# Four edits to the prologue of an attention and mixture-of-experts kernel: an earlier turn of the first maxima, loads from another queue, a split table load, twenty unread products

## The chip, the cores and the metric

The kernel runs on one core of a Trainium2 chip. The metric is the device time of one execution in microseconds (us); lower is better. An execution is read through a hardware profile of the same program: what each engine did and when, what the DMA queues moved, and the clock that TensorE was granted.

## The reference

Two layers over x of shape (2, 1024, 128) in f32. Only the first is touched by the change: self-attention with 16 heads of 8 dimensions and a distance bias that falls with the head.

```python
qkv = x @ qkv_w.T + qkv_b                      # split per head into q, k, v of 8 columns
scores = einsum('bhid,bhjd->bhij', q, k) / sqrt(8) - |i - j| * 0.5**h
out = einsum('bhij,bhjd->bhid', softmax(scores), v) @ out_w.T + out_b
x = layernorm(x + out)
# second layer: layernorm, attention over pairs of tokens, top-2 of 8 experts
# with capacity 640 (gelu between two matmuls), weighted sum, residual, layernorm
```

## The kernel before

**Units.** The first attention is cut into 32 units (`UNITS`), each a few heads by some blocks of 128 queries; the first 24 have two heads. A unit's scores are computed twice. First come its eight "rows" (`max_half`): TensorE writes 128 queries by 1024 keys into a pair of PSUM banks (two pairs alternate), and VectorE reduces each pair to a row maximum (`reduce_row`). Then the scores are computed again, turned round, with the maxima subtracted inside the matmul (`exp_half`), ScalarE takes the exponent, and TensorE multiplies by the values (`values`). q and k are held as three bf16 parts, so that a product has 72 rows, to which rows for the distance and for the maxima are added. The diagonal block gets its distances from one more 128-column product with `slope_eye`.

**How maxima reach the second pass.** GpSimd splits a unit's eight maxima into three bf16 parts (`split_max`), VectorE turns the tile (`swap_max`), and SP's queue writes it to DRAM, waits until it has landed and loads it into rows of `q_stacks` (`load_max`). Unit 0 of the main loop starts when this is there, when unit 2's stacks are loaded, and when a pair of banks is free.

**The prologue.** TensorE turns the weights and x and makes eight projections (`project(y)`, 512 columns of f32). Pieces 0 to 2 go straight from SBUF into unit 0's stacks (`first_copies`, half of the copies from GpSimd's queue, half from SP's). Then TensorE waits, and runs the rows of units 0 and 1 (16 rows) with projections 4 to 7 and some weight transposes between them (`first_work`, after rows 3, 5, 7, 9 and 11). ScalarE evicts each projection in two operations (`project`, L1218 and L1224), and then copies the turned weights. VectorE's order is written out at the file's end: eight rows of unit m+2, with the turn of unit m+1's maxima after row index 2 of them. SP loads units 1 and 2 (`load_parts`, each two loads of q and two of k through DRAM) and then, in the loop, unit m+3 at unit m. GpSimd loads all slopes behind heads 0 to 3 in one transfer (L841) before it splits unit 0's maxima.

**The main loop.** For each of eight j, TensorE runs one row of unit m+2 and two halves of exponent input of unit m; after the second four it multiplies by the values. Waits are counted semaphores; every queue is in program order.

Of the kernel before, what the change touches and what calls it, by code (L numbers as in the profile page):

```python
# [12 lines left out]
P = 128  # L13
S = 2
N = 1024
D = 128
H = 16
DH = D // H
# [11 lines left out]
PARTS = 3  # L30
PRODUCTS = PARTS * PARTS * DH
# [4 lines left out]
SLOTS = 4  # L36
# [8 lines left out]
UNITS_C = H // 2  # L45
UNITS = NT // TC * UNITS_C
# [7 lines left out]
FOURS = 24  # L54
# [16 lines left out]
WEIGHT_DMAS = 4  # L71
FILLS = EXPERTS + TOP * NT // 8
SCATTERS = 2
LAST_GROUPS = ((0, 2), (2, 4), (4, 8), (8, 12), (12, 14), (14, 16))


# [100 lines left out]
def heads_in(m):  # L177

    return 4 if m >= FOURS else 2


def head_of(m, e):

    n = heads_in(m)
    u = m % (H // n)
    return 2 * n * (u // 2) + 2 * e + u % 2


def first_block(m):

    return NB // 2 + NB // 4 * ((m - FOURS) // SLOTS) if m >= FOURS else NB // 2 * (m // UNITS_C % 2)
# [17 lines left out]
def loads_by(m):  # L209

    return sum(loads_of(k) for k in range(m % SLOTS, m + 1, SLOTS))


def body(nc, t):

    with ExitStack() as ctx:
# [3 lines left out]
        def sem(name):  # L220
            return ctx.enter_context(nc.semaphore(name))
# [24 lines left out]
        k_late = sb("k_late", [P, H // 2, N], BF16)  # L246
# [66 lines left out]
        y_to = [sb(f"y_to{u}", [P, CT], U32) for u in range(2)]  # L313

        ld_w, ld_bias, ld_const, ld_slopes = sem("ld_w"), sem("ld_bias"), sem("ld_const"), sem("ld_slopes")
        ld_x = [sem(f"ld_x{g}") for g in range(NT // 4)]
        w_turned, w_kept = sem("w_turned"), sem("w_kept")
        x_turned, x_kept = sem("x_turned"), [sem(f"x_kept{g}") for g in range(NT // 4)]
# [74 lines left out]
        def queries(m, e):  # L393
            n = N // heads_in(m)
            return q_stacks[:, m % SLOTS, n * e:n * (e + 1)]

        def max_pair(k):

            first_bank = RING + 2 * (k % 2)
            return ps[:, first_bank:first_bank + 2, :]  # L400
# [15 lines left out]
        def first_copies(y, e):  # L416
# [3 lines left out]
            for i in range(PARTS):  # L420
# [4 lines left out]
                else:  # L425
                    yield k_stacks[to, 0, e, HALF * half:HALF * (half + 1)], parts[rows, y, :, :]

        def fetch_group(eng, g):

            lo, hi = LAST_GROUPS[g]  # L430
            eng.dma_start(got[:, lo:hi, :], yt.rearrange("(a p k) d -> p a (k d)", p=P, k=TOP)[:, lo:hi, :]
                          ).then_inc(fetched[g], 16)
# [17 lines left out]
        def _(sp):  # L450
# [15 lines left out]
                for out, src in first_copies(y, 1):  # L466
                    sp.dma_start(out, src).then_inc(loaded_direct, 16)

            def stack_of_four(m, rows):
                k = m % SLOTS  # L470
                if k < 2:
                    return k_late[rows, 4 * k:4 * (k + 1), :]
                return k_stacks[rows, 2 * (k - 2):2 * (k - 1), :, :].rearrange("r k e n -> r (k e) n")

            def load_tables(m):
                slot, n, h = m % SLOTS, heads_in(m), head_of(m, 0)
                if m < FOURS:
# [8 lines left out]
                if m >= FOURS or m % UNITS_C < SLOTS:  # L486
# [1 line left out]
                    sp.dma_start(q_stacks[ROW_ALIBI:ROW_MAX, slot, :].rearrange("r (e n) -> r e n", e=n),  # L488
                                 t["c_alibi_q"][:, first:first + N // n].unsqueeze(1).broadcast_to(
                                     [ROW_MAX - ROW_ALIBI, n, N // n])).then_inc(loaded[slot], 16)  # L490

            def load_parts(m):
                slot, s, n = m % SLOTS, m // (2 * UNITS_C), heads_in(m)
                first = P * first_block(m)
                for e in range(n):
                    sp.dma_start(queries(m, e)[0:PRODUCTS],
                                 q_dram[s, head_of(m, e), :, :, first:first + N // n].rearrange(
                                     "p d n -> (p d) n").unsqueeze(1).broadcast_to([PARTS * DH, PARTS, N // n])
                                 ).then_inc(loaded[slot], 16)
                    if n == 2:  # L500
                        sp.dma_start(k_stacks[0:PRODUCTS, slot, e, :],
                                     k_dram[s, head_of(m, e)].rearrange("d p n -> (d p) n").unsqueeze(0).broadcast_to(
                                         [PARTS, PARTS * DH, N])).then_inc(loaded[slot], 16)
                if FOURS <= m < FOURS + SLOTS:
                    h = head_of(m, 0)
                    for i in range(PARTS):
                        sp.dma_start(stack_of_four(m, slice(PARTS * DH * i, PARTS * DH * (i + 1))),
                                     k_dram[s, h:h + 7:2].rearrange("e d p n -> (d p) e n")).then_inc(loaded[slot], 16)

            def load_max(m):  # L510

# [31 lines left out]
                first_stack(y)  # L543
            for b in range(3):
                sp.wait_ge(parts_saved[b], SAVED[b])
            load_parts(1)
            load_parts(2)
            load_max(0)

            for m in range(UNITS):  # L550
                for c in range(LAST):
                    if m == first_unit(c + 1) + 1:
                        load_heads(c, 0, units_of(c) // 2)
                if m + 3 < UNITS:
                    if m > 0:
                        sp.wait_ge(ring_full, EXP_PLACE[m - 1, NB - 1, 1] + 1)
                    if m + 3 == UNITS_C:
                        sp.wait_ge(parts_saved[3], SAVED[3])
                    if m + 3 == 2 * UNITS_C:
                        sp.wait_ge(rest_saved, 16 * sum(1 if piece(y)[1] else PARTS for y in range(4, 8)))  # L560
                    load_tables(m + 3)
                    load_parts(m + 3)
                if m + 1 < UNITS:
                    load_max(m + 1)
                if m % 2 == 0 and m >= 2:
                    send_out(m // 2 - 1)
# [38 lines left out]
        def _(pool):  # L605
# [11 lines left out]
            for k in range(SLOTS):  # L617
                r = k % 2
# [46 lines left out]
            def split_max(m):  # L665
                b = m % 2
                src, rst, out = row_max[:, b, :], max_rest[:, b, :], max_parts[:, b, :]
                pool.wait_ge(mx_used, NB * m + NB)
                if m >= 2:
                    pool.wait_ge(max_swapped, m - 1)  # L670
                pool.tensor_tensor(out[:, 0:NB], src, no_bits[:], ALU.add).then_inc(split, 1)  # L671
                pool.wait_ge(split, 3 * m + 1)
                pool.tensor_tensor(rst, src, out[:, 0:NB], ALU.subtract).then_inc(split, 1)
                pool.wait_ge(split, 3 * m + 2)
                pool.tensor_tensor(out[:, NB:2 * NB], rst, no_bits[:], ALU.add).then_inc(split, 1)
                pool.wait_ge(split, 3 * m + 3)
                pool.tensor_tensor(out[:, 2 * NB:3 * NB], rst, out[:, NB:2 * NB], ALU.subtract).then_inc(max_split, 1)
# [160 lines left out]
            copy_v(1)  # L838
            copy_v(2)
            split_rest(3)  # L840
            pool.dma_start(slope_eye[:, 4:H, :], t["c_slope_eye"][4:H].rearrange("h p n -> p h n")).then_inc(ld_slopes, 16)  # L841
            split_max(0)
            split_rest(4)
            split_max(1)
            for m in range(UNITS):
# [30 lines left out]
        def _(pe):  # L876
# [219 lines left out]


            pe.wait_ge(ld_const, 16 * 3)
            pe.wait_ge(x_kept[3], 1)
            pe.wait_ge(first_loaded, 16 * 3 * PARTS)  # L1100
            pe.wait_ge(loaded[0], 16 * TABLES)
# [14 lines left out]
            pe.wait_ge(qf_ready, 8)  # L1116

            for m in range(UNITS):
                for group in range(2):
                    half = 2 * m + group  # L1120
                    for j in range(GROUP * group, GROUP * (group + 1)):
                        if j % 2 == 0:
                            for stage, c in hooks(half, (j % GROUP // 2,)):
                                late(stage, c)
                        if j == 0:
                            pe.wait_ge(max_loaded[m % SLOTS], 16 * turn_of(m))
                            if m + 2 < UNITS:
                                pe.wait_ge(loaded[(m + 2) % SLOTS], 16 * loads_by(m + 2))
                        if m + 2 < UNITS:
                            for h in range(2):  # L1130
                                max_half(m + 2, j, h)
                        for e in range(2):
                            exp_half(m, j, e)
                    for stage, c in hooks(half, (2,)):
                        late(stage, c)
                    if group == 1:
                        values(m, 0, half)
                    elif m > 0:
                        values(m - 1, 1, half)
# [65 lines left out]
        def _(act):  # L1205
# [50 lines left out]
            project(3)  # L1256
            act.wait_ge(loaded_direct, 16 * 3 * PARTS)
            act.wait_ge(first_loaded, 16 * 3 * PARTS)
            for y in range(4, 8):
                project(y)  # L1260
            act.wait_ge(late_turned, 1)
            act.copy(wo_t[:], ps[:, LATE_BANK, 0:P]).then_inc(late_kept, 1)
            act.copy(wq_t[:], ps[:, LATE_BANK, P:3 * P]).then_inc(late_kept, 1)
# [126 lines left out]
        def _(dve):  # L1390
# [277 lines left out]
            for m in range(-2, UNITS):  # L1668
                for i in range(NB):
                    if m + 2 < UNITS:  # L1670
                        reduce_row(m + 2, i)
                    if i == 2 and 0 <= m + 1 < UNITS:
                        swap_max(m + 1)
                    if i % GROUP == GROUP - 1 and m >= 0:
                        for stage, c in hooks(2 * m + i // GROUP):
                            late(stage, c)
# [147 lines left out]
```

## Time and profile before

| | us |
|---|---|
| median of 3 runs (606.59 to 613.73) | 608.09 |
| the profiled execution | 611.53 |
| its span, first to last instruction | 609.5 |
| TensorE busy | 525.3 (86% of the span) |
| VectorE busy | 404.4 (66%) |
| ScalarE busy | 340.3 (56%) |
| GpSimd busy | 216.9 (36%) |

Times in the profile run from the start of the span. PE is TensorE, DVE VectorE, ACT ScalarE, POOL GpSimd, SP the queue of SyncE; PEld is TensorE's weight load. A name with q behind it (SPq, ACTq) is an engine's DMA issue. In the chain of work that ended last, TensorE holds 71% of the span and VectorE 14%. TensorE's mean granted clock is 0.934 of full speed: 1.00 is 2.4 GHz and 0.50 is 1.2 GHz.

### The profile page before, as it was taken

To read this page: it belongs to the slowest core of one execution; us is meant where nothing else is said; L and a number is where in the kernel's file an instruction comes from. 1 tells how busy PE (TensorE), PEld (TensorE's weight loads), DVE (VectorE), ACT (ScalarE), POOL (GpSimd) and SP (SyncE) were. 2 spreads that over 40 slices of the span, in tenths; PEclk is the share of its full clock that TensorE was granted. 3 is DMA by queue.
4 is the path that set the end of the run, shared out by engine and by line. 5 is a ranking of instruction groups with operands and counts; after the bars stand their busy time and mean duration, and the time that the engine had idled before them with its cause. 6 is when DMAs were issued, how large, how long until landed. Compare 5 with 4: busy or idle time off the path is not lost.

```text
span 609.5 us, 11848 instructions
## 1 busy us (share of the span) xinstructions
PE 525.3 (86%) x4506; PEld 297.5 (49%) x4506; DVE 404.4 (66%) x688; ACT 340.3 (56%) x666; POOL 216.9 (36%) x404
## 2 busy tenths in 40 slices
PE   6579999999999999999999999999995219999910
PEld 4234444444444554544455455555663107888710
DVE  2697777787888667798865779987767612222217
ACT  4147676676767777756776676578691002332404
POOL 5735453111225215014701500470032740645540
PEclk9798999999999999999999999999997558999975
DMA  7622342322322323122222421111000121442124
GB/s 159 178 82 74 75 135 66 100 89 92 104 83 72 93 75 119 50 83 72 65 58 57 112 68 58 47 38 31 3 20 17 37 61 46 129 135 81 55 83 140
DMA packets 49191, 47.89 MB, mean 79 GB/s; under 512 B 13251, under 2 KB 38709, under 8 KB 49136
## 3 DMA queue, kind: packets, MB, share of 16 engines
q1 hardware_dynamic: 40800, 31.93, 19.0%
q0 software_dynamic: 5488, 12.73, 6.7%
q10 hardware_dynamic: 2848, 2.49, 1.3%
q8 instruction: 35, 0.57, 0.4%
q14 instruction: 20, 0.16, 0.1%
HBM read 31.67 MB, written 16.06 MB: 78 GB/s over the span
## 4 chain that ended last, share of the span: by engine, by line
PE 71%; DVE 14%; DMA 6%; POOL 3%; issue 3%; ACT 1%; another core or an unknown queue 1%; POOLq 0%; ACTq 0%; DVEq 0%; SPq 0%
PE ps L944 33%; PE ps L1004 17%; DVE row_max L1440 8%; PE ps L1160 6%; PE ps L1172 5%; PE ps L946 4%; POOL xd L831 2%; DMA max_dram<-max_turned 1%; DVE heads L1511 1%; PE ps L1044 1%; DVE x_tok L1730 1%; DMA k_stacks<-k_late 1%; PE ps L1149 1%; DMA q_stacks<-max_dram 1%
## 5 line engine op out<-in xcount | busy, mean ns | idle before, releaser
L1440 DVE TENSOR_REDUCE row_max<-ps 128x1 f32<-128x1024 f32 x256 | 297.3, 1213 | 89.7 <-PE ps L944 46.7
L1277 ACT ACTIVATE probs<-ps 128x512 f32<-128x512 f32 x512 | 268.3, 606 | 88.6 <-PE ps L946 47.1
L944 PE MATMUL ps<-k_stacks,q_stacks 96*128 96x512 bf16 x448 | 145.4, 389 | 12.8 <-DMA k_stacks<-k_late 5.9
L944 PE MATMUL ps<-q_stacks,k_stacks 99*128 99x512 bf16 (+1 forms) x512 | 142.4, 355 | 0.9 <-ACT probs L1277 0.5
L1004 PE MATMUL ps<-probs,v_unit 128*32 128x256 f32 x2048 | 123.8, 382 | 0.0
L946 PE MATMUL ps<-distance,slope_eye 128*128 128x128 bf16 x512 | 110.7, 222 | 0.0
L1004 PEld LDWEIGHTS ps<-probs,v_unit 128*32 128x32 f32 x2048 | 60.0, 109 | 51.5 <-issue 9.6
L944 PEld LDWEIGHTS ps<-k_stacks,q_stacks 96*128 96x128 bf16 x448 | 39.5, 99 | 82.0 <-DVE row_max L1440 28.3
L944 PEld LDWEIGHTS ps<-q_stacks,k_stacks 99*128 99x128 bf16 x512 | 48.7, 98 | 41.6 <-ACT probs L1277 12.1
L946 PEld LDWEIGHTS ps<-distance,slope_eye 128*128 128x128 bf16 x512 | 50.5, 99 | 25.8 <-issue 1.9
L1361 ACT ACTIVATE probs<-ps 128x640 f32<-128x640 f32 x32 | 22.5, 703 | 64.9 <-PE ps L1160 62.6
L867 POOL DMA_INDIRECT yt<-prod_mix,y_to x40 | 38.9, 972 | 52.9 <-DVE prod_mix L1699 41.9
L671 POOL TENSOR_TENSOR max_parts<-row_max,no_bits 128x8 bf16<-128x8 f32 x32 | 6.5, 202 | 130.7 <-DVE row_max L1440 128.7
L661 POOL COPY v_unit<-v_all 128x128 f32<-128x128 f32 (+1 forms) x28 | 8.5, 313 | 120.6 <-PE ps L1004 120.6
L1160 PE MATMUL ps<-probs,w 128*128 128x320 f32 x128 | 38.3, 455 | 1.2 <-DVE probs L1687 1.2
L831 POOL DMA_INDIRECT xd<-row_of,slot_u x32 | 31.8, 993 | 12.4 <-issue 11.0
L1172 PE MATMUL ps<-w,probs 128*128 128x128 f32 x280 | 32.4, 275 | 0.0
L1172 PEld LDWEIGHTS ps<-w,probs 128*128 128x128 f32 x280 | 31.8, 192 | 0.0
L1160 PEld LDWEIGHTS ps<-probs,w 128*128 128x128 f32 x128 | 24.1, 200 | 12.4 <-ACT probs L1361 3.3
L1686 DVE COPY columns<-probs 128x10 f32<-128x10 f32 x8 | 1.3, 164 | 37.5 <-PE ps L1149 30.8
L944 PE MATMUL ps<-q_stacks,k_late 99*128 99x256 bf16 x128 | 20.7, 272 | 0.0
L944 PE MATMUL ps<-k_late,q_stacks 96*128 96x512 bf16 x64 | 19.2, 381 | 1.2 <-DVE row_max L1440 1.2
(250 smaller groups left out, 444.4 us busy)
## 6 DMA issues: line engine op xcount, KB each, us to landing
k_stacks<-k_dram SPq DMA_DIRECT2D x46, 144.0 KB
q_stacks<-q_dram SPq DMA_DIRECT2D x46, 72.0 KB
w<-in_w SPq DMA_DIRECT2D x12, 256.0 KB
xd<-blank POOLq DMA_DIRECT2D x8, 325.0 KB, 2.8
probs<-xd SPq DMA_DIRECT2D x8, 325.0 KB
k_stacks<-in_c_alibi_k SPq DMA_DIRECT2D x24, 96.0 KB
out_dram<-out_t SPq DMA_DIRECT2D x16, 128.0 KB
yt<-zeros POOLq DMA_DIRECT2D x4, 512.0 KB, 3.0
```

The source lines that it names most:

```text
L661: pool.tensor_copy(v_unit[:, slot, :, 0:n, DH * r:DH * (r + 1)], v_all[:, first:first + 2 * n - 1:2, :, :].rearrange("p e j d -> p j e d") ...
L671: pool.tensor_tensor(out[:, 0:NB], src, no_bits[:], ALU.add).then_inc(split, 1)
L831: pool.indirect_dma_start(out=xd, out_offset=bass.IndirectOffsetOnAxis(ap=slot_u[c][:, k, j:j + 1], axis=0), in_=row_of[k][:, tiles(c)[j], ...
L867: pool.indirect_dma_start(out=yt, out_offset=bass.IndirectOffsetOnAxis(ap=y_to[u][:, a:a + 1], axis=0), in_=y_out[u][:, a, :], in_offset=N ...
L944: mm = pe.matmul(out, lhs, rhs, start=True, stop=at is None)
L946: mm = pe.matmul(out[:, at:at + P], slope_eye[:, head_of(m, e), :], distance[:], start=False, stop=True)
L1004: mm = pe.matmul(ps_o[32 * c:32 * c + 32, :], v_unit[:, m % SLOTS, j, c * heads_in(m) // 4, :], probs[:, (NB * m + j) % KEPT, QUARTER * c: ...
L1160: mm = pe.matmul(ps[:, 2 + 2 * (f % 2) + h, 0:CAP // 2], w1[u][:, f * P:(f + 1) * P], x_in_t[u][:, h * CAP // 2:(h + 1) * CAP // 2], start ...
L1172: mm = pe.matmul(ps[:, 6 + a // 4, (a % 4) * P:(a % 4 + 1) * P], act_t[u][:, f, a * P:(a + 1) * P], w2[u][:, f, :], start=(f == 0 and a % ...
L1277: act.activation(probs[:, k % KEPT, HALF * e:HALF * (e + 1)], ps[:, ring_of(n), :], ACT.Exp).then_inc(ring_read, 1)
L1361: act.activation(act_t[u][:, f, :].rearrange("p (h n) -> p h n", h=2), ps[:, 2 + 2 * (f % 2):4 + 2 * (f % 2), 0:CAP // 2], ACT.Gelu).then_ ...
L1440: dve.tensor_reduce(row_max[:, m % 2, i:i + 1], max_pair(k).rearrange("p a n -> p (a n)"), AX.X, ALU.max).then_inc(mx_used, 1)
```

## The change

Four edits, all ahead of the main loop or at its first passes.

1. `swap_max(0)` is called after the first row of unit 1 instead of the third.
2. `load_parts(2)` leaves SP's queue. ScalarE issues its four DMAs between `project(6)` and `project(7)`, behind a wait for unit 1's loads.
3. The slopes of heads 4 to 7 are loaded where heads 4 to 15 were; those of heads 8 to 15 after `split_max(0)`, and TensorE waits for them at unit 2 of the loop.
4. TensorE runs twenty 128x512 bf16 products into a PSUM bank that nothing reads, ahead of the waits for unit 0's stacks.

```diff
+IDLE_TURNS = 20
...
             for b in range(3):
                 sp.wait_ge(parts_saved[b], SAVED[b])
-            load_parts(1)
-            load_parts(2)
+            load_parts(sp, 1)
             load_max(0)
...
             split_rest(3)
-            pool.dma_start(slope_eye[:, 4:H, :], t["c_slope_eye"][4:H].rearrange("h p n -> p h n")).then_inc(ld_slopes, 16)
+            pool.dma_start(slope_eye[:, 4:8, :], t["c_slope_eye"][4:8].rearrange("h p n -> p h n")).then_inc(ld_slopes, 16)
             split_max(0)
+            pool.dma_start(slope_eye[:, 8:H, :], t["c_slope_eye"][8:H].rearrange("h p n -> p h n")).then_inc(ld_last_slopes, 16)
             split_rest(4)
...
             pe.wait_ge(ld_const, 16 * 3)
+            for _ in range(IDLE_TURNS):
+                pe.matmul(max_pair(0)[:, 0, :], distance[:], slope_eye[:, 0:4, :].rearrange("p h n -> p (h n)"),
+                          start=True, stop=True)
             pe.wait_ge(x_kept[3], 1)
...
             for m in range(UNITS):
+                if m == 2:
+                    pe.wait_ge(ld_last_slopes, 16)
...
-            for y in range(4, 8):
+            for y in range(4, 7):
                 project(y)
+            act.wait_ge(loaded[1], 16 * loads_by(1))
+            load_parts(act, 2)
+            project(7)
...
-                    if i == 2 and 0 <= m + 1 < UNITS:
+                    if i == (0 if m < 0 else 2) and 0 <= m + 1 < UNITS:
                         swap_max(m + 1)
```

`load_parts` and `stack_of_four` are moved out of SP's block unchanged, with the issuing engine as an argument.

## Rows read from the trace of the kernel before

**Rows 1.** Chain that ended last, 0 to 120 us: start us, length us, what.

```profile
24.64 0.59 PE ps L944
...
31.34 8.01 DVE row_max L1440 x7
39.50 1.97 DMA max_dram<-max_turned
41.48 2.58 DMA q_stacks<-max_dram
44.07 0.35 issue
```

**Rows 2.** Stretches: busy us (instructions) of PE, PEld, DVE, ACT, POOL; clock, DMA share, GB/s.

```profile
18.80:24.60 5.80, 0.00 (x0) 0.00 (x0) 1.17 (x6) 1.30 (x2) 5.36 (x10) 0.91 0.71 203
24.60:30.60 6.00, 5.60 (x14) 2.04 (x15) 4.70 (x4) 0.00 (x0) 2.08 (x3) 0.51 0.64 186
39.40:44.40 5.00, 2.67 (x13) 0.86 (x13) 5.00 (x6) 1.11 (x6) 2.30 (x4) 0.97 0.41 113
44.40:50.90 6.50, 6.48 (x23) 2.87 (x24) 4.43 (x5) 3.00 (x6) 5.04 (x13) 0.50 0.22 68
70.00:130.00 60.00, 59.01 (x536) 27.36 (x533) 45.50 (x45) 41.31 (x82) 20.24 (x43) 1.00 0.36 100
```

**Rows 3.** Timeline, VectorE: start us, length us, instruction [idle before, releaser].

```profile
25.79 4.82 DVE L1440 TENSOR_REDUCE row_max<-ps 128x1 f32<-128x1024 f32 x4 [5.82 <-PE ps L944]
...
39.39 5.71 DVE L1440 TENSOR_REDUCE row_max<-ps 128x1 f32<-128x1024 f32 x5
...
51.38 5.75 DVE L1440 TENSOR_REDUCE row_max<-ps 128x1 f32<-128x1024 f32 x5 [0.41 <-PE ps L944]
```

**Rows 4.** Timeline, TensorE: end of the x work, a projection at either clock.

```profile
16.70 2.02 PE L895 MATMUL ps<-w_t,qkv 128*128 128x128 f32 x16 [1.21 <-ACT qkv L1252]
...
29.14 1.67 PE L888 MATMUL ps<-qkv,w_t 128*128 128x512 f32 x2
...
31.64 1.02 PE L888 MATMUL ps<-qkv,w_t 128*128 128x512 f32 x2
```

**Rows 5.** Timeline, ScalarE and GpSimd: last evictions, copies, splits, DMA issues.

```profile
36.04 0.62 ACT L1224 CAST k_late<-heads 128x512 bf16<-128x512 f32 x1
37.58 0.69 ACT L1218 ACTIVATE heads<-ps,bias_q_scaled 128x512 f32<-128x512 f32 x1 [0.93 <-PE ps L888]
...
40.16 0.38 ACT L1268 COPY wv_t<-ps 128x64 f32<-128x64 f32 x2
...
25.62 1.06 POOL L841 DMA_DIRECT2D slope_eye<-in_c_slope_eye  x1
...
36.88 0.20 POOL L677 TENSOR_TENSOR max_parts<-max_rest,max_parts 128x8 bf16<-128x8 f32 x1
```

**Rows 6.** Timeline, SP's queue: issues of the units' loads.

```profile
24.11 0.79 SPq L496 DMA_DIRECT2D q_stacks<-q_dram  x1
...
29.68 0.71 SPq L501 DMA_DIRECT2D k_stacks<-k_dram  x1
...
42.28 0.51 SPq L478 DMA_DIRECT2D k_stacks<-in_c_alibi_k  x1
...
56.42 0.79 SPq L496 DMA_DIRECT2D q_stacks<-q_dram  x1
```

**Rows 7.** Short stretches: length, clock, DMA share, GB/s.

```profile
37.00:38.00 1.00, 1.00 0.09 33
38.00:39.00 1.00, 1.00 0.00 0
...
62.50:63.00 0.50, 1.00 0.20 74
...
64.00:64.50 0.50, 1.00 0.01 1
```

**Rows 8.** Chain, 78 to 96 us: the slowest trip of the maxima.

```profile
86.50 6.63 DMA max_dram<-max_turned
```

More of the change, by code:

```diff
@@ L315, in body @@
         ld_w, ld_bias, ld_const, ld_slopes = sem("ld_w"), sem("ld_bias"), sem("ld_const"), sem("ld_slopes")
+        ld_last_slopes = sem("ld_last_slopes")
         ld_x = [sem(f"ld_x{g}") for g in range(NT // 4)]
@@ L426, in first_copies, with stack_of_four, load_parts @@
                     yield k_stacks[to, 0, e, HALF * half:HALF * (half + 1)], parts[rows, y, :, :]
+        def stack_of_four(m, rows):
+            k = m % SLOTS
+            if k < 2:
+                return k_late[rows, 4 * k:4 * (k + 1), :]
+            return k_stacks[rows, 2 * (k - 2):2 * (k - 1), :, :].rearrange("r k e n -> r (k e) n")
+        def load_parts(eng, m):
+            slot, s, n = m % SLOTS, m // (2 * UNITS_C), heads_in(m)
+            first = P * first_block(m)
+            for e in range(n):
+                eng.dma_start(queries(m, e)[0:PRODUCTS],
+                             q_dram[s, head_of(m, e), :, :, first:first + N // n].rearrange(
+                                 "p d n -> (p d) n").unsqueeze(1).broadcast_to([PARTS * DH, PARTS, N // n])
+                             ).then_inc(loaded[slot], 16)
+                if n == 2:
+                    eng.dma_start(k_stacks[0:PRODUCTS, slot, e, :],
+                                 k_dram[s, head_of(m, e)].rearrange("d p n -> (d p) n").unsqueeze(0).broadcast_to(
+                                     [PARTS, PARTS * DH, N])).then_inc(loaded[slot], 16)
+            if FOURS <= m < FOURS + SLOTS:
+                h = head_of(m, 0)
+                for i in range(PARTS):
+                    eng.dma_start(stack_of_four(m, slice(PARTS * DH * i, PARTS * DH * (i + 1))),
+                                 k_dram[s, h:h + 7:2].rearrange("e d p n -> (d p) e n")).then_inc(loaded[slot], 16)
         def fetch_group(eng, g):
@@ L467, in first_stack @@
                     sp.dma_start(out, src).then_inc(loaded_direct, 16)
[L469 to L473, printed above, removed]
             def load_tables(m):
@@ L490, in load_tables @@
                                      [ROW_MAX - ROW_ALIBI, n, N // n])).then_inc(loaded[slot], 16)
[L492 to L508, printed above, removed]
             def load_max(m):
@@ L561, in _ @@
                     load_tables(m + 3)
-                    load_parts(m + 3)
+                    load_parts(sp, m + 3)
                 if m + 1 < UNITS:
```

## The prediction
> **What bounds the kernel now.** I read the page first: TensorE is busy for 86% of the span and holds 71% of the chain, so the middle is TensorE's. The windows by stretch say the same: 59.0 of 60 us busy from 70 to 130 us, at full clock [rows 2]. A loop so full starts later or sooner as a block, so what the prologue gives up passes on to the end nearly whole. Next I read the chain through the prologue. It enters the rows of unit 0 at 24.6 us, goes through the rows of units 0 and 1 at VectorE's pace, and then through the trip of unit 0's maxima: save 1.97 us, load 2.58, 0.35 of issue, so that TensorE enters the main loop at 44.07 + 0.35 = 44.42 us [rows 1]. Last I read the clock. It is 0.91 on average in the 5.8 us in which TensorE does nothing and 0.51 from 24.6 to 30.6. It falls again to 0.50 from 44.4 to 50.9 us, after five microseconds in which TensorE was busy for 2.67 of 5.00 [rows 2]. The reader is to see two prices: a late entry into the loop, and a slow first half unit behind it.
>
> **The unread products.** The last work on x ends at 16.70 + 2.02 = 18.72 us [rows 4], the first row starts at 24.64 [rows 1]. A product streams 512 columns: 0.213 us at 2.4 GHz, 0.427 at 1.2 GHz (columns over clock). Twenty take 4.3 us, to 23.0, and hide in the wait; wholly at the low clock they take 8.5, to 27.3, and cost 2.6. A mean clock of 0.91 over 5.8 us is a full one until about 23.6 although TensorE had stopped at 18.7 [rows 2], so I take 4.3 and cost them at nothing.
>
> What they buy: a row streams 512 + 128 + 512 columns, 0.96 us at the low clock and 0.48 at the full one. The first reduction started 25.79 - 24.64 = 1.15 us after the row [rows 1, 3]; at full clock 0.67, so 25.3. Reductions then follow at 8.01 / 7 = 1.144 us [rows 1]. The fifth would start at 25.3 + 4 x 1.144 = 29.9 us, against 31.34. It is fed in time: row 3 may start when row 1 is reduced, at 27.6; 0.48 for it, 1.02 for the projection behind it [rows 4], 0.67 for the next gives 29.8. **Gain 1.45 us.** If the clock is low again by then, the same sum is 27.6 + 0.96 + 1.67 + 1.15 = 31.4, gain nothing. TensorE works 3 rows x 0.48 in the first 2.5 us after 24.6, a poor load like the one before 44.4. I keep 0 and 1.45 as bounds and take 1.0 for the mean of executions; the sum below goes by 1.45, and says what the lower value does.
>
> **The turn two rows sooner.** Before, the eighth row is reduced at about 31.34 + 4 x 1.144 = 35.9, GpSimd's split starts right behind it and ends at 36.88 + 0.20 = 37.08 [rows 5], and the turn comes only at 39.3, just ahead of the reductions of 39.39 [rows 3]. After, it waits for the split alone: all 1.45 sooner, split done 35.65, ninth reduction done 35.7, turn done 35.9. VectorE stalls some 0.1 us, since the ninth reduction just covers the split. The save starts at 35.95 instead of 39.50, lands at 37.9, and the load at 40.5; with 0.35 of issue TensorE could start at 40.9. So this edge stops being the last. The next one late is the bank pair: unit 2's first row needs the reduction of the row two before, the fifteenth. Before, the sixteenth ended at 39.39 + 5.71 = 45.10, the fifteenth at 43.95; less 1.45 and plus the stall gives **42.6**, a gain of 1.8 if nothing else is later.
>
> **Unit 2's loads.** Here something is later. ScalarE ends `project(6)` at 36.04 + 0.62 = 36.66, now 35.2 [rows 5]. Four issues at SP's 0.79 [rows 6] take it to 38.3. `project(7)` and the weight copies follow; before they took from 37.58 to 40.16 + 0.38 = 40.54, 2.96 us [rows 5], so 41.3 us now, 1.3 under the 42.6 at which TensorE needs them. Hidden. But the loads themselves: unit 4's, alone, were issued from 56.42 and its traffic ended just before 64.0 [rows 6, 7], 7.4 us. From 35.2 that is **42.6 at the soonest**. Before, the same loads were issued by 29.68 + 0.71 and gone by 37.4 [rows 6, 7], 7 us ahead of their use; that slack is spent. And they aren't alone. GpSimd's second slopes load and its save of piece 4 fall into the stretch, and, since SP's `load_max(0)` is done 3.5 us sooner, SP goes on to unit 3's tables and loads at 39 instead of 42.28 [rows 6]. Units 1 and 2 together took 24.1 to 37.4, 13.3 us for two, so overlapping units delay each other: an extra of 0 to, at the extreme, 13.3 - 7.4 = 5.9 us. Unit 3's own large loads come only in the last two microseconds, so I take 1.0, near the lower end: landed 43.6, and with 0.35 of issue TensorE enters the loop at **43.95 instead of 44.42**. If the clock spoiled the first stretch, everything is 0.4 later and the entry is where it was.
>
> A transfer tail of this kind shows a DMA share of 0.20 at 74 GB/s [rows 7], that is about 3 of 16 engines: a k load runs on few engines, and adding another queue doesn't widen it. The Trainium skill, page "DMA: Bandwidth & Descriptors", section "Why a DMA increments its semaphore by 16 and not by 1", says that a copy is spread over the largest count up to 16 that divides its slowest dimension, the lowest-numbered engines first; k's is 3. The trace agrees with three.
>
> **The rest.** The second slopes issue costs GpSimd under the 1.06 us of the whole one [rows 5]; behind it stand `split_rest(4)` and then `split_max(1)`, which can't start before the sixteenth reduction. From 39.40 to 44.40 GpSimd was busy for 2.30 of 5.00 us [rows 2], so 2.7 us of idle time cover it. Hidden; without that cover unit 1's maxima would come 1.06 later, and they are wanted a whole unit after unit 0's. TensorE's wait for the last slopes is at loop unit 2, near 70 us, 30 us after the issue. Nothing.
>
> **Sum.** Entry 44.42 to 43.95: -0.5. Slow half unit behind it: unchanged. Span 609.5 to 609.0, the profiled execution 611.53 to 611.0. The median shown is 608.09, 3.4 below the profiled execution, so the same difference gives **607.6 us**.
>
> **Rivals.** (a) *The second slow stretch goes.* In the loop's first steps TensorE streams four products of 512 columns and three of 128, 2.03 us at 1.2 GHz and 1.01 at 2.4; at the low clock it sets the pace, at the full one VectorE does. The reduction of the loop's fourth row started at 51.38; at 1.144 us a row it would start at 45.1 + 3 x 1.144 = 48.5 [rows 3]. So 2.85 us hang on the clock. If the load lands at 42.6 the entry is 43.0, 1.4 sooner, and TensorE's lean stretch is shorter: -1.4 - 2.85 = -4.2, **603.9**. For it: the mean of 0.97 over the lean stretch [rows 2] says that the clock held for nearly all of it, and the cure comes with a small shift. Against: by my entry the lean stretch grows, from 5 us to nearly 6, since it now begins 1.45 sooner and ends only 0.5 sooner. Chance 0.25. A mild form, start sooner and clock kept in one execution of two, is about 605.5 and lies between.
>
> (b) *The loads make the entry later: slower.* Place: engines that carry unit 2's k, unit 3's first loads and the small load of the maxima at once. The slowest save of the maxima took 6.63 us instead of 1.97, with unit loads and weights in flight [rows 8]. Price: the entry is at load + 0.35, so it turns into a loss when unit 2's traffic needs more than 44.07 - 35.2 = 8.9 us, or when save and load together need more than 44.07 - 35.95 = 8.1 against 4.55 before. With 6.63 + 2.58 the entry is at 45.5, +1.1; with the load 3 us delayed, 46.0, +1.5: **609.4**. Chance 0.2. The same page of the Trainium skill, section "Queues, rings and completion order", says that an engine takes turns between its queues by whole packets of descriptors; were that so here, the many short pieces of the maxima would stand behind pieces of unit 2's k, and this rival is what it would give. No row of before has the two on different queues.
>
> (c) *The products are in the way.* If the clock is already low at 18.7, they end near 27.3 and the first row is 2.6 late: **610.5** after the 0.1 to 0.2 that comes back. Chance 0.05.
>
> (d) *Nothing passes on*, since the load alone sets the entry and takes all: 608.1. Chance 0.05.
>
> **Numbers.** My forecast, entry within about 1 us of before, has 0.45: its own range is 606.6 to 608.6. The range holds (a)'s nearer part and (b): 603.7 to 610.3, with (c) and the far side of (a) outside. A change of 2% is 12 us, about what a measurement of this kernel can tell from none; no case above comes near it, so faster 0.02, same 0.96, slower 0.02.
>
> **What would show it.** In the profile after: twenty products from 18.7 to 23.0 and a clock of 1.00 at 24.6 (else the first step is wrong); the fifth reduction at 29.9; the save of the maxima at 36.0; ScalarE's four issues from 35.2; and, as the release of the first row of the loop, a DMA of unit 2's stacks and not of the maxima, at 43.6. If the release is a reduction at 42.6, the loads were quick, and I was too dark; if the clock then holds at 1.00 from 44 to 51 us, (a) holds and the gain is about 4 us.

## The result: slower by 0.4%, and the profile after

The changed kernel takes 611.49 us at the median against 608.64 us, and the ratio is 1.0041 with an interval of 1.0023 to 1.0058, some 2.5 us. The forecast was 607.6 us, a gain of 0.5 us on the median known then. The profiled execution took 611.57 us, its span is 609.6 us, so the two profiled executions end alike: that of before was 2.9 us slower than its median, that of after was at its median. The two traces differ where the change is, and the difference can be followed from there to the end of the loop. The first view is the chain that ended last, cut to the prologue (start us, length us, what).

```profile
19.63 4.32 PE ps L1102 x20
23.94 0.67 issue
...
28.70 1.71 PE ps L890 x2
...
36.10 0.62 ACT k_late L1231
36.72 0.75 ACTq L440
...
39.11 8.91 DMA k_stacks<-k_dram
48.02 0.24 issue
48.26 0.58 PE ps L946
```

The twenty products take 4.3 us and end before the first row, as worked out. TensorE enters the loop at 48.26 us instead of 44.42 [rows 1], and what releases it is neither the trip of the maxima nor a reduction but unit 2's second k load, issued by ScalarE at 39.11 and landed 8.91 us later. From the first of the four issues to the landing it is 48.02 - 36.10 = 11.9 us; the same loads alone took 7.4 [rows 6, 7]. The queues' timeline shows who else was there, first ScalarE's queue and then SP's.

```profile
36.10 1.36 ACTq L440 DMA_DIRECT2D q_stacks<-q_dram  x1
...
39.11 0.73 ACTq L445 DMA_DIRECT2D k_stacks<-k_dram  x1
39.89 0.69 ACT L1225 ACTIVATE heads<-ps,bias_q_scaled 128x512 f32<-128x512 f32 x1 [3.17 <-issue]
```

```profile
37.42 0.37 SPq L516 DMA_DIRECT2D max_dram<-max_turned  x1
38.98 0.76 SPq L518 DMA_DIRECT2D q_stacks<-max_dram  x1
39.78 0.48 SPq L498 DMA_DIRECT2D k_stacks<-in_c_alibi_k  x1
...
42.06 0.71 SPq L445 DMA_DIRECT2D k_stacks<-k_dram  x1
...
43.63 0.71 SPq L445 DMA_DIRECT2D k_stacks<-k_dram  x1
```

Since the maxima turn sooner, SP is through with them at 39.7 us and goes on at once to unit 3: its two k loads are issued at 42.06 and 43.63, while both of unit 2's are on their way. Unit 3 is not wanted for another unit. The short stretches (length, clock, DMA share, GB/s) show what they share.

```profile
43.00:44.00 1.00, 1.00 0.85 275
44.00:45.00 1.00, 0.99 0.62 183
45.00:46.00 1.00, 0.50 0.25 94
46.00:47.00 1.00, 0.50 0.21 80
47.00:48.00 1.00, 0.50 0.19 74
```

A lone unit's load ends in a tail at a share of 0.20 and 74 GB/s [rows 7]. Here two units from two queues are in flight, and the tail is the same 0.20: the second queue adds no rate. From 46 to 48 us the traffic by queue (packets, MB, share of 16 engines; q1 is SP's, q0 GpSimd's, q10 ScalarE's) is:

```profile
q1 hardware_dynamic: 52, 0.08, 10.6%
q0 software_dynamic: 19, 0.05, 6.2%
q10 hardware_dynamic: 15, 0.02, 3.2%
```

The three together make up the 20%: SP's unit 3 and transfers of GpSimd take most of it, and the load that TensorE waits for gets the least. Unit 3's tail goes on alone to 50.9 us.

The timeline of VectorE (start, length, instruction, what ended the idle time) has the rest.

```profile
25.30 4.66 DVE L1450 TENSOR_REDUCE row_max<-ps 128x1 f32<-128x1024 f32 x4 [4.44 <-PE ps L946]
31.40 5.75 DVE L1450 TENSOR_REDUCE row_max<-ps 128x1 f32<-128x1024 f32 x5 [1.44 <-PE ps L946]
37.19 0.21 DVE L1458 STREAM_TRANSPOSE max_turned<-max_parts 128x32 bf16<-128x32 bf16 x1
...
49.42 1.23 DVE L1450 TENSOR_REDUCE row_max<-ps 128x1 f32<-128x1024 f32 x1 [4.13 <-PE ps L946]
...
54.01 5.71 DVE L1450 TENSOR_REDUCE row_max<-ps 128x1 f32<-128x1024 f32 x5
```

VectorE waits 4.13 us for the loop. The first row starts at a slightly different time in each execution, so I compare kernels by the time from the first reduction of all to the fourth reduction of the loop. Before it is 51.38 - 25.79 = 25.6 us [rows 3], after 54.01 - 25.30 = 28.7: **3.1 us lost in the prologue**. That is carried through: the last save of the maxima is issued at 442.74 us, 388.7 us after the fourth reduction, and before at 440.14, 388.8 after it. Between the loop and the end the profiled execution won back 2.5 us in work that no edit touches; the median did not.

The stretches of before, asked of after (busy us and instructions of PE, PEld, DVE, ACT, POOL; clock, DMA share, GB/s):

```profile
24.60:30.60 6.00, 4.69 (x15) 1.87 (x16) 4.66 (x4) 0.07 (x1) 3.79 (x6) 0.78 0.43 120
39.40:44.40 5.00, 2.95 (x16) 0.99 (x14) 5.00 (x6) 2.31 (x8) 3.21 (x5) 1.00 0.61 179
44.40:50.90 6.50, 2.64 (x10) 1.27 (x11) 2.11 (x2) 0.95 (x2) 4.86 (x13) 0.54 0.24 83
70.00:130.00 60.00, 58.97 (x554) 27.55 (x552) 44.73 (x44) 40.33 (x80) 22.63 (x47) 1.00 0.36 98
```

Against [rows 2], the first stretch has a clock of 0.78 instead of 0.51, the third has TensorE busy for 2.64 of 6.50 us instead of 6.48, and the loop is what it was.

### The profile page after: what moved, and what is told of

The parts are those of the page before. It is cut to its first block, busy times and chain, and to the rows that moved or that the text cites. A ratio compares the mean times of both kernels' runs of the same rounds, so it can differ in the third digit from the quotient of the medians.

```text
span 609.6 us, 11889 instructions
## 1 busy us (share of the span) xinstructions
PE 526.7 (86%) x4526; PEld 298.3 (49%) x4526; DVE 403.9 (66%) x688; ACT 340.2 (56%) x666; POOL 218.7 (36%) x405
## 4 chain that ended last, share of the span: by engine, by line
PE 70%; DVE 14%; DMA 6%; issue 3%; POOL 3%; ACT 2%; ACTq 0%; POOLq 0%; DVEq 0%; SPq 0%
PE ps L946 32%; PE ps L1006 16%; DVE row_max L1450 8%; PE ps L1167 6%; PE ps L1179 5%; PE ps L948 4%; POOL xd L832 2%; DMA k_stacks<-k_dram 1%; DVE heads L1521 1%; PE ps L1046 1%; DMA max_dram<-max_turned 1%; DVE x_tok L1740 1%; DMA w_nat<-in_qkv_w 1%; PE ps L1156 1%; PE ps L890 1%
## 5 line engine op out<-in xcount | busy, mean ns | idle before, releaser
L946 PE MATMUL ps<-k_stacks,q_stacks 96*128 96x512 bf16 x448 | 143.7, 386 | 12.3 <-DVE row_max L1450 5.5
L869 POOL DMA_INDIRECT yt<-prod_mix,y_to x40 | 38.9, 973 | 49.9 <-DVE prod_mix L1709 36.1
```

Source lines behind the costliest of these rows:

```text
L869: pool.indirect_dma_start(out=yt, out_offset=bass.IndirectOffsetOnAxis(ap=y_to[u][:, a:a + 1], axis=0), in_=y_out[u][:, a, :], in_offset=N ...
L946: mm = pe.matmul(out, lhs, rhs, start=True, stop=at is None)
```

## The experiments

Theory one: the loss is unit 2's loads alone. Their last issue is at 39.1 us instead of 29.7, and they share a few DMA engines with unit 3's loads, which the earlier turn of the maxima pulls forward. Theory two: the turn, the slopes, the products or ScalarE's queue as such cost the time. All ratios are to the kernel before on the same chip.

**Unit 2's loads back on SP's queue**, the other three edits kept.

```diff
             load_parts(sp, 1)
+            load_parts(sp, 2)
...
-            for y in range(4, 7):
-                project(y)
-            act.wait_ge(loaded[1], 16 * loads_by(1))
-            load_parts(act, 2)
-            project(7)
+            for y in range(4, 8):
+                project(y)
```

> The changed kernel with unit 2's loads back on SP's queue; the other three edits stay. Theory one (the late, shared loads of unit 2 are the whole loss): the first row of the loop is released by the reduction of the fifteenth row at about 42.6 to 43.5 us instead of by a DMA at 48.0, and the time falls 4 to 5 us below the changed kernel's, to a ratio of 0.992 to 0.998 of the kernel before. Theory two (the loss comes from the earlier turn, the split slopes or the products): the entry stays later than 44.4 us and the ratio at 1.002 or above.

Measured: 0.9984 (0.9966 to 1.0003), 5.7 thousandths below the changed kernel. The loss is gone; theory one holds for its place. The gain of 0.2% to 0.8% that I expected did not come whole. TensorE enters the loop at 42.59 us, where I expected it, but the first reduction was early too, at 23.99: between the two are 18.6 us, as in the kernel before. The timelines of VectorE and, last line, TensorE say why.

```profile
23.99 9.14 DVE L1448 TENSOR_REDUCE row_max<-ps 128x1 f32<-128x1024 f32 x8 [3.86 <-PE ps L947]
34.35 1.23 DVE L1448 TENSOR_REDUCE row_max<-ps 128x1 f32<-128x1024 f32 x1 [1.22 <-PE ps L947]
...
49.12 5.75 DVE L1448 TENSOR_REDUCE row_max<-ps 128x1 f32<-128x1024 f32 x5
```

```profile
33.64 0.39 PE L947 MATMUL ps<-k_stacks,q_stacks 96*128 96x512 bf16 x1 [1.19 <-DMA k_stacks<-k_dram]
```

Eight reductions now run without a gap, 9.14 us for eight; the products do keep the clock here. But the ninth row waits 1.2 us for unit 1's load: the rows have caught up with it. SP's save of the maxima, issued at 35.72, is followed by the load only at 38.92, 3.2 us for the save, with unit 2's loads ahead of it; it did not set the entry, since TensorE was still at the sixteenth row until 42.5 us. From the first reduction to the loop's fourth it is 25.1 us.

**Only ScalarE's issue of unit 2's loads**, on the kernel before.

```diff
+            act.wait_ge(loaded[1], 16 * loads_by(1))
+            load_parts(act, 2)
```

> The kernel before with one edit only: ScalarE's queue issues unit 2's loads between projections 6 and 7. Theory one: issue from 36.7 us, unit 3's loads follow 3 us later than in the changed kernel, so the overlap is smaller; landed at 44.5 to 47, entry at 45 to 47.5 and a ratio of 1.001 to 1.005. Theory two (this edit alone is harmless, since 7.4 us from 36.7 is 44.1, under the 44.07 of before or nearly): entry within 0.3 us of 44.42, ratio 1.000 +- 0.001.

Measured: 1.0066 (1.0047 to 1.0085), more than the whole change and more than either theory gave it. One edit makes the loss, and the other three win some of it back. The chain of this kernel:

```profile
40.10 3.45 DMA max_dram<-max_turned
43.57 2.81 DMA q_stacks<-max_dram
```

Here it was not the load of unit 2 that came last but the trip of the maxima: 6.3 us instead of 4.6 [rows 1], although nothing else was in SP's queue. The entry is at 46.76 us. So the late loads hurt in a second way: the small transfers of the maxima get slower beside them. That they share DMA engines with them is the likely reason; the trace doesn't name the engines of a single transfer. The trace gives 28.3 us to the loop's fourth reduction, 2.7 more than before; the ratio says 4 us, and that difference I can't place.

**Unit 3's loads held back** until unit 2's have landed, in the changed kernel.

```diff
+                    if m == 0:
+                        sp.wait_ge(loaded[2], 16 * loads_by(2))
                     load_tables(m + 3)
```

> The changed kernel with one wait more: SP holds unit 3's tables and loads back until unit 2's have landed. Theory one in its form that the two units' k loads share the same few DMA engines: unit 2's last load lands 7.4 to 8.8 us after the first issue, at 43.5 to 45, instead of 11.9 us after; entry at 44 to 45.3, 3 to 4 us sooner than in the changed kernel. Theory two (ScalarE's queue is slow by itself, or the slopes and the save of piece 4 are what it shares with): landing stays at 46 or later, entry 46.5 to 48.

Measured: 1.0029 (1.0014 to 1.0043). The queues and TensorE:

```profile
35.82 0.37 SPq L516 DMA_DIRECT2D max_dram<-max_turned  x1
40.13 0.76 SPq L518 DMA_DIRECT2D q_stacks<-max_dram  x1
42.49 0.32 SPq L498 DMA_DIRECT2D k_stacks<-in_c_alibi_k  x1
```

```profile
44.31 0.58 PE L948 MATMUL ps<-k_stacks,q_stacks 96*128 96x512 bf16 x1 [2.17 <-DMA q_stacks<-max_dram]
```

ScalarE's first issue was at 33.72, and at 42.49 unit 2 had landed: 8.8 us at most instead of 11.9. So unit 3's loads were 3 us of the delay, as theory one has it. Then the second way shows alone: the save takes 4.3 us and the load 3.8, and they set the entry at 44.31. GpSimd's new slopes load is issued 1.4 us ahead of this save and is a rival for its slowness. Two things speak against it: the run before this one has no such load and its save takes 3.45 us, and in five of the runs below, with cut k loads, the slopes load stands 0.3 us ahead of the save, which takes 1.4 to 2.0 us. Without unit 3 in the way the change is still no gain.

**Each k load cut into three transfers of 24 rows**, on all two-head units of the changed kernel (counts of awaited loads raised to match). A k load writes 72 rows from a source repeated three times, an outer size of 3.

```diff
-                    eng.dma_start(k_stacks[0:PRODUCTS, slot, e, :],
-                                 k_dram[...].unsqueeze(0).broadcast_to([PARTS, PARTS * DH, N]))
+                    for i in range(PARTS):
+                        eng.dma_start(k_stacks[PARTS * DH * i:PARTS * DH * (i + 1), slot, e, :],
+                                     k_dram[s, head_of(m, e)].rearrange("d p n -> (d p) n")
+                                     ).then_inc(loaded[slot], 16)
```

> The changed kernel with each k load of the two-head units (72 rows, a source repeated three times) cut into three transfers of 24 rows, on all units. Theory one in its form that a k load runs on three of sixteen engines because its outer size is 3: the pieces run on more engines, a unit's traffic has no tail at a DMA share of 0.20, and unit 2's last piece lands soon after its issue. ScalarE then has eight issues of 0.75 us, 36.1 to 42.3 us, so landing and the weight copies put the entry at 44.5 to 45.5 instead of 48.26. Theory two (bytes or the queue limit the load): landing stays near 48 or gets later, and the tail at 0.20 remains.

Measured: 0.9953 (0.9933 to 0.9973). The same queue, the same bytes and the same order of issues on every queue, and the loss turns into a gain of 2.9 us. Short stretches, then TensorE and ScalarE's queue:

```profile
41.00:42.00 1.00, 0.86 0.93 260
42.00:43.00 1.00, 0.50 0.49 173
43.00:44.00 1.00, 0.50 0.55 159
44.00:45.00 1.00, 0.50 0.06 21
```

```profile
41.88 0.58 PE L946 MATMUL ps<-k_stacks,q_stacks 96*128 96x512 bf16 x1 [0.55 <-DVE row_max L1450]
```

```profile
37.15 2.10 ACTq L446 DMA_DIRECT2D k_stacks<-k_dram  x3
```

Both units' traffic is over by 44 us, but for a share of 0.06 in the next, with no tail at 0.20, and the entry is released by the reduction at 41.88, the step that I had worked out at 42.6. I had expected the eight issues to run from 36.1 to 42.3 us and the entry at 44.5 to 45.5. They ran from 33.69 to 39.25: 0.6 us shorter together, and 2.4 us sooner, since in this execution the clock held and the rows went by without a gap. So part of the distance between this trace and that of after is the clock and not the cut. The run without the twenty products, below, takes it out: its first rows are as slow as those of after (fifth reduction 6.0 and 6.1 us after the first), its k loads are cut, and it enters the loop 18.9 us after its first reduction instead of 23.0.

The Trainium skill, page "DMA: Bandwidth & Descriptors", section "Why a DMA increments its semaphore by 16 and not by 1", says that a copy runs on the largest number of engines up to 16 that divides the slowest dimension of both its sides. The traces agree for an outer size of 3, where a share of 0.20 of 16 engines is 3. For 24 that would be 12 engines; the traces don't single that number out, since the shares above hold transfers of GpSimd too. They show that it is more than 3: from 42 to 43 us SP's queue alone has 34% of the 16 engines, where three would be 19%.

**The same cut with unit 2's loads on SP's queue.**

> The k loads cut into three transfers of 24 rows, unit 2's loads on SP's queue, the other three edits as in the changed kernel. If the few DMA engines under a k load were the whole trouble, the queue no longer matters: entry into the loop at 41.9 us by a reduction as with ScalarE's queue, ratio 0.995 +- 0.0015. If ScalarE's queue had a merit of its own (unit 1's loads not sharing with unit 2's), row 0 of unit 1 waits here for unit 1's loads, by up to 1 us, and the ratio is 0.996 to 0.998.

Measured: 0.9966 (0.9954 to 0.9979); the first nine reductions run without a gap, 10.27 us for nine. The interval overlaps that of ScalarE's queue: once the loads are wide, the queue makes no difference that these runs can tell, and no row waits for unit 1's loads on either. The profiled execution was this kernel's fastest, 604.05 us against a median of 606.21, so its trace looks better than the kernel is.

**The cut alone, on the kernel before.**

> The kernel before, with nothing but the k loads cut into three transfers of 24 rows. Theory one (the cut only takes away what the change had made late): in the kernel before, unit 2's loads had 7 us of slack and the entry hung on the trip of the maxima, so the prologue is as it was: entry at 44.4, ratio 0.999 to 1.000; a gain in the loop, at the trip of 86.5 us (6.63 us for the save), of at most 1 to 2 us would make it 0.997. Theory two (the cut is itself the gain of the run with both): ratio 0.995.

Measured: 0.9982 (0.9966 to 0.9999), about 1.1 us. As theory one wanted, the entry hangs on what it hung on before (45.17, released by the load of the maxima, with the save at 1.98 and the load at 2.58 us); the loop's fourth reduction comes 25.0 us after the first, 0.6 sooner. The gain that I can place is in the loop: from that reduction to the last save of the maxima it is 387.7 us, and 388.8 before. It is 387.7 to 388.1 in all eight kernels with cut loads and 388.2 to 389.1 in the six others. So of the 2.9 us of the run above some 1.1 are the cut's own, in the loop, and the rest is the four edits'. The slow trip of before [rows 8] is one place to look; the same save in this kernel, and its load behind it:

```profile
85.94 0.35 SPq L515 DMA_DIRECT2D max_dram<-max_turned  x1
89.75 0.74 SPq L517 DMA_DIRECT2D q_stacks<-max_dram  x1
```

3.8 us instead of 6.63, and TensorE is busy for 59.94 us of the 60 from 70 to 130 instead of 59.01 [rows 2].

**Without the twenty products**, cut kept.

> The changed kernel with cut k loads and without the twenty unread products. Theory one (the products keep the clock at full for the first rows): without them the clock is 0.5 from about 24.6 to 31 us, the fifth reduction starts 1 to 1.5 us later after the first than with them, the entry moves from 41.9 to 42.9 to 43.4, ratio 0.997 to 0.998. Theory two (the reductions set the pace whatever the clock): entry within 0.3 us of 41.9, ratio 0.995.

Measured: 0.9952 (0.9928 to 0.9976), the same as with them, as theory two has it. VectorE's timeline shows the first rows at the low clock:

```profile
24.36 4.82 DVE L1447 TENSOR_REDUCE row_max<-ps 128x1 f32<-128x1024 f32 x4 [5.06 <-PE ps L946]
30.36 5.75 DVE L1447 TENSOR_REDUCE row_max<-ps 128x1 f32<-128x1024 f32 x5 [1.18 <-PE ps L946]
```

The fifth reduction comes 6.0 us after the first, against 4.57 where they run without a gap, and the entry is at 43.25 instead of 41.88. Theory one was right on the place, not on the ratio. It isn't seen in the time, since in this execution the clock was low for 3.4 us around the entry and not 6.8: from the first reduction to the loop's fourth it is 24.6 against 24.5 us.

**The products alone**, on the kernel before.

> The kernel before with the twenty unread products and nothing else. If they keep the clock in the first rows, the fifth reduction starts up to 1.2 us sooner after the first than in the kernel before, and the whole trip of the maxima with it: entry at 43.2 to 44.2, ratio 0.997 to 0.999. If the loads of units 1 and 2 then bind (both are in flight until 37.4), or the clock falls all the same, ratio 0.999 to 1.001.

Measured: 0.9995 (0.9977 to 1.0013). What the products win, unit 1's loads take back. TensorE's timeline:

```profile
35.46 0.61 PE L944 MATMUL ps<-k_stacks,q_stacks 96*128 96x512 bf16 x1 [2.57 <-DMA k_stacks<-k_dram]
```

Row 0 of unit 1 waits 2.6 us for a k load, and comes back at the low clock. So it was the second case that I had named, the loads of units 1 and 2.

**The late turn**, in the changed kernel with cut loads.

> The changed kernel with cut k loads, and unit 0's maxima turned after the third row of unit 1 again. Theory one (with the loads out of the way, the trip of the maxima is the next limit): save 2.2 us later than with the early turn, at 37.2, load landed at 41.5 to 42.5, entry at 41.9 to 42.9 against 41.9; ratio 0.995 to 0.998. Theory two (the early turn is needed): entry at 44 or later, ratio 0.999 or above.

Measured: 0.9989 (0.9970 to 1.0007) against 0.9953, with intervals that just touch: the early turn is worth some 2 us once the loads are wide. Two kernels whose first rows were at the low clock as here (without the products, and with one slopes transfer) come to 24.6 and 24.7 us; here the fourth reduction is 26.4 us after the first. It was worse than I had thought: I expected an entry of 41.9 to 42.9, and it was at 44.48. The save was issued at 38.67 instead of 37.2, and it took 2.9 us, although the k loads were cut.

**The slopes in one transfer**, in the changed kernel with cut loads.

> The changed kernel with cut k loads and the slopes of heads 4 to 15 in one transfer again. If their bytes compete with unit 1's loads, row 0 of unit 1 waits for a DMA and the entry is 0.5 to 1 us later, ratio 0.996 to 0.997; if they are covered, ratio 0.995 +- 0.001 and the entry at 41.9 +- 0.3 from the same start of the rows.

Measured: 0.9967 (0.9950 to 0.9985), not to be told from 0.9953. From the first reduction it is 19.0 us to the entry, against 17.4 with the split, but all 1.6 us of that are the first rows at the low clock (fifth reduction after 6.13 us instead of 4.57). No row waits for unit 1's loads.

**Two more products after each of rows 11 to 15**, in a bank that nothing reads, with cut loads, once for each queue.

```diff
                     first_work(NB * m + i)
+                    if NB * m + i >= 11:
+                        if NB * m + i == 11:
+                            pe.wait_ge(qf_ready, 7)
+                        for _ in range(2):
+                            pe.matmul(ps[:, 7, :], distance[:], slope_eye[:, 0:4, :]..., start=True, stop=True)
```

> The kernel with cut k loads and unit 2's loads on SP's queue, with two more unread products of 512 columns after each of rows 11 to 15 of the prologue, in a bank that nothing reads (ps 7, behind a wait for ScalarE's seventh eviction). Theory one (the lean rows ahead of the loop let the clock fall): the clock holds at 1.00 from 40 to 52 us, the loop's first four reductions are 1.15 us apart instead of 2.03, and the time falls 2 to 3 us below the same kernel without them, ratio 0.990 to 0.992. Theory two (the clock falls anyway, or the products are in the rows' way): ratio within 0.001 of that kernel's or above it.

> The changed kernel (unit 2's loads on ScalarE's queue) with cut k loads and two unread products after each of rows 11 to 15 of the prologue. If the lean rows are what lets the clock fall ahead of the loop, the clock holds from 40 to 52 us as it did with SP's queue, the loop's fourth reduction starts at 45 to 46.5 us instead of 48.92, and the ratio is 0.991 to 0.993; if ScalarE's late copies or the loads bind in their place, 0.994 to 0.996.

Measured: 0.9933 (0.9909 to 0.9957) with SP's queue and 0.9940 (0.9918 to 0.9962) with ScalarE's, the two fastest kernels here. The stretches around the entry with SP's queue (columns as above), and VectorE:

```profile
39.40:44.40 5.00, 4.85 (x26) 1.90 (x25) 5.00 (x6) 0.48 (x5) 2.36 (x4) 1.00 0.60 174
44.40:50.90 6.50, 6.34 (x37) 2.68 (x36) 6.50 (x8) 6.27 (x12) 5.73 (x14) 1.00 0.15 51
```

```profile
36.38 11.42 DVE L1454 TENSOR_REDUCE row_max<-ps 128x1 f32<-128x1024 f32 x10
```

The clock holds at 2.4 GHz through both stretches, and ten reductions across the entry run without a gap. From the ninth reduction to the loop's fourth it is about 12.8 us on either queue, against 14.0 without these products on SP's queue and 15.4 on ScalarE's: 1.2 and 2.5 us. That is what the traces show. From the first reduction the traces gain less or nothing (table below), because in both warm kernels the clock fell in the first rows. On ScalarE's queue the fourth reduction came at 49.28 us and not at 45 to 46.5. In the time it is 0.3% below the same kernel without them with SP's queue and 0.1% with ScalarE's, less than theory one had, and the intervals overlap: the step is shown, its price only roughly.

Fourteen traces side by side, first reduction to the loop's fourth, with the change in time that the ratio gives at 608.6 us:

| kernel | us | by the ratio |
|---|---|---|
| before | 25.6 | 0 |
| after | 28.7 | +2.5 |
| loads on SP | 25.1 | -1.0 |
| only ScalarE's issue | 28.3 | +4.0 |
| unit 3 held | 27.1 | +1.8 |
| products alone | 26.2 | -0.3 |
| cut k alone | 25.0 | -1.1 |
| change, cut k | 24.5 | -2.9 |
| the same, on SP | 23.1 | -2.1 |
| the same, no products | 24.6 | -2.9 |
| the same, late turn | 26.4 | -0.7 |
| the same, one slopes transfer | 24.7 | -2.0 |
| cut, SP, warm | 23.5 | -4.1 |
| cut, ScalarE, warm | 24.0 | -3.6 |

With 1.1 us taken off where k is cut (the gain in the loop), the first column less 25.6 gives the second to within 1.5 us. So a difference of under 1.5 us between two traces says little about the kernels; the clock in the first rows alone makes 1.2 to 1.7 (the fifth reduction comes 4.57 us after the first in some kernels with the twenty products, 5.79 to 6.25 in others).

## Why the prediction was wrong, step by step

- **What bounds the kernel.** Right. The loop passed the loss on: 388.7 and 388.8 us from its fourth reduction to its last save.
- **The unread products.** Right in place and length: they ran from 19.6 to 23.9 us against 18.7 to 23.0, in front of a first row at 24.61. Of what they buy, both bounds were met. Where the clock held, eight reductions ran without a gap and the fifth came after 4.57 us instead of 5.55. In the profiled execution of after the clock fell at 27.9 us and the fifth came at 31.40 instead of the 29.9 of the sum. Of the ten traces with the twenty products five are of the first kind and five of the second; the four without them are all slow (5.55 to 6.26 us). In the time no gain of theirs shows: 0.9995 alone, and 0.9952 without them against 0.9953 with.
- **The turn two rows sooner.** The step was right: the split took 1.05 us behind the eighth reduction and the turn followed at once; the save was issued at 37.42 instead of 35.95, by the lost 1.45. Its worth was missed, because a later edge covered it here. With cut loads it is worth 2 us.
- **Unit 2's loads: the step that failed.** I had named the load as the edge that comes last, and got its size wrong. The sum had 7.4 us alone and an extra of 0 to 5.9, of which I took 1.0, because unit 3's own large loads come only in the last two microseconds. The extra was 4.5 us (11.9 less 7.4). The held-back run shows that some 3 us of it were unit 3's loads; the other 1.4 stayed with unit 3 out of the way, and GpSimd's transfers, which are in the same tail, are the likely part of it, not taken apart by a run. The reason stood in my own text: a tail at a share of 0.20 means three engines. Unit 3's two k loads are 144 KB each; at the tail's 74 GB/s they take some 4 us, my estimate after the fact, and that is what an overlap can cost, from either queue. I used the share to say that a queue doesn't widen a load, and not to price the overlap. The rest of the way to 48.26 is 0.9 us by which ScalarE's first issue came later (36.10 instead of 35.2): `project(6)` ended 1.5 us later than in the sum, since the clock had fallen, and the issue began 0.6 us before that end.
- **The slow half unit behind the entry** was to be unchanged. It was 1.2 us shorter: from the entry to the loop's fourth reduction 5.75 us instead of 6.96, so 4.3 us lost up to the entry, counted from the first reduction, became 3.1.
- **The rest.** Right: ScalarE's copies ended at 42.2 us, 1 us after the time worked out, and nothing waited for them; neither GpSimd's second issue nor the wait at unit 2 shows up.
- **The rivals.** (b), slower through the shared engines, is what happened, and it got 0.2. Its point of decision was right, 8.9 us from the first issue; its price of +1.5 us at the entry was less than half of the 3.8 measured. Its second half, the maxima delayed by unit 2's loads on another queue, did not set the entry in the changed kernel, but did in two of the runs: 6.3 and 8.1 us of save and load instead of 4.6. (a) did not occur: with so late an entry the clock had fallen already at 45 us. Its price was about right: the 2.85 us that it hung on the clock are 2.5 in the kernel with cut loads on ScalarE's queue, once the two products behind rows 11 to 15 hold the clock.
- **The range** ended at 610.3 and the median was 611.49. It took one half of rival (b) at a time. The trace of before allowed more: 5.9 us of extra was my own upper bound for the load, and I didn't carry it into the range.

What stays open: why the ratio of ScalarE's issue alone is 1.3 us more than its trace shows, and how much each short trip of the maxima loses to which transfer. The second would need the DMA engines of single transfers to be seen.

## What to carry to other kernels

Before a load is moved to a later time or to another queue, read its tail: a DMA share that stays at 0.20 of 16 engines says that it runs on three, and here two such loads in flight at once took each other's time although they were on two queues. A repeated source with a small outer size can be cut into transfers whose outer size is larger, for the same bytes and little issue time. When an edit frees a queue sooner, ask what that queue does next, since here it was a load that nobody wanted yet. A slack of 7 us in front of a load is not free to spend; it is what kept the load's rate from mattering.

## What I had not expected of the hardware

- Cutting a 72-row, three-times repeated load into three of 24 rows took its end from a share of 0.20 to shares of 0.49 and 0.55, of which SP's queue alone had 0.34. Units 2 and 3 were through some 10.5 us after ScalarE's first issue (near 44.2 less 33.69) instead of 14.8 (50.9 less 36.10). Three issues took 1.2 to 2.1 us.
- Transfers of 6 and 8 KB got slower beside another queue's traffic. Save and load of the maxima took 1.97 and 2.58 us in the kernel before [rows 1], 3.45 and 2.81 with ScalarE's uncut loads in flight, and 4.3 and 3.8 in the kernel with unit 3 held. Beside cut loads the save took 1.4 to 2.0 us, but 2.9 in the kernel with the late turn.
- The clock fell while TensorE was at work too. In the kernel with cut loads on SP's queue it went from 2.4 to 1.2 GHz at about 41.6 us, in the loop's first row; in the five microseconds before, TensorE was busy for 3.05 and no gap was longer than 0.56. In the same kernel with two more unread products behind rows 11 to 15 it was busy for 4.85 of 5.00 us, and the clock stayed at 2.4 GHz.
- DMA issues on ScalarE's queue keep its work waiting. The four took 1.36, 0.76, 0.80 and 0.73 us; the first ran beside the last cast (36.10 to 36.72), and the next activation then waited 3.17 us.
